# Graph attention softmax: the carry into a row's first and last run by two operations with tables of 16-bit penalties instead of a second pair of scans

## The reference

```python
q = (x @ Wq + bq).reshape(n, H, C)          # n = 6250, H = 4, C = 64
kj = (x @ Wk + bk).reshape(n, H, C)[src] + (edge_attr @ We).reshape(-1, H, C)
vj = (x @ Wv + bv).reshape(n, H, C)[src] + (edge_attr @ We).reshape(-1, H, C)
logits = einsum('ehc,ehc->eh', q[dst], kj) / sqrt(C)
m = segment_max(logits, dst)
ex = exp(logits - m[dst])
a = ex / (segment_sum(ex, dst)[dst] + 1e-16)
agg = segment_sum(vj * a, dst).reshape(n, H * C)
h = relu(agg + x @ Ws + bs)                  # and the same once more on h, without relu
```

## Time and profile before

| what | value |
|---|---|
| time, median of 3 runs | 4497.03 us (4490.62 to 4498.63) |
| the profiled execution's own time | 4498.7 us |
| its span, from first to last instruction | 4496.9 us |
| busy share of the span | PE 91%, DVE 84%, ACT 68%, POOL 71% |
| DMA | 237 GB/s mean, about 250 GB/s in the attention passes |

### The profile page before, as it was taken

How to read it: one execution, slowest core, us unless ns; L and a number is a source line. 1 busy time by engine, 2 the same in 40 slices (tenths; PEclk the granted TensorE clock), 3 DMA queues, 4 the chain that set the end, 5 groups by cost and what they waited for, 6 DMA issues and landing times. The chain is left out here.

```text
span 4496.9 us, 108726 instructions
## 1 busy us (share of the span) xinstructions
PE 4109.7 (91%) x17720; PEld 3175.0 (71%) x17720; DVE 3759.8 (84%) x20610; ACT 3036.2 (68%) x10782; POOL 3210.1 (71%) x3078
## 2 busy tenths in 40 slices
PE   5999999998979999999999998979999999999996
PEld 4887877775657777777777775557777777777764
DVE  5655555556979999999999998889999999999996
ACT  2333333333518988889898895139999999999983
POOL 6777777773067888778787782188888888888842
PEclk9999999999999999999999999999999999999999
DMA  5887887774678888888888884588888888888855
GB/s 171 255 250 236 247 242 241 237 234 134 204 235 257 260 257 256 255 253 258 259 261 250 253 265 122 181 253 259 259 255 255 257 258 255 256 259 256 260 156 160
DMA packets 770941, 1064.81 MB, mean 237 GB/s; under 512 B 111323, under 2 KB 588728, under 8 KB 770277
## 3 DMA queue, kind: packets, MB, share of 16 engines
q0 software_dynamic: 171184, 540.40, 40.1%
q1 hardware_dynamic: 599094, 517.47, 38.1%
HBM read 906.27 MB, written 151.16 MB: 235 GB/s over the span
## 5 line engine op out<-in xcount | busy, mean ns | idle before, releaser
L1476 POOL DMA_INDIRECT e_kv<-kv,src x1664 | 1662.6, 999 | 536.7 <-issue 301.1
L1709 ACT ACTIVATE e_vals<-e_kvj,e_ex 128x65 f32<-128x65 f32 x6572 | 1686.7, 334 | 0.1
L1497 PE MATMUL e_q<-q,e_pick 128*128 x3328 | 1056.2, 399 | 144.7 <-DVE e_logit L1604 113.7
L1604 DVE CUSTOM_DVE_ANT_0 e_kvj<-e_kvj,e_q 128x64 f32<-128x64 f32 x6656 | 1062.7, 215 | 4.3 <-PE e_q L1497 0.4
L153 POOL DMA_INDIRECT rows_x<-x_rows,rows_src x783 | 745.2, 952 | 243.5 <-issue 174.3
L1497 PEld LDWEIGHTS e_q<-q,e_pick 128*128 128x128 f32 x3328 | 576.6, 190 | 434.7 <-issue 369.4
L1539 PE MATMUL e_sum<-e_vals,e_mask 128*128 128x260 f32 x2536 | 784.8, 391 | 20.4 <-ACT e_vals L1709 9.4
L1592 DVE TENSOR_TENSOR e_kvj<-e_kv,e_e 128x512 f32<-128x512 f32 x1110 | 752.8, 678 | 54.9 <-DMA e_kv<-kv,src 28.6
L1487 PE MATMUL e_e<-e_we,e_ea 112*128 112x256 f32 x2220 | 670.6, 383 | 39.4 <-DMA e_ea<-attr_tiles 39.3
L1468 POOL TENSOR_SCALAR e_pick<-e_spots,own 128x512 f32<-128x512 bf16 x416 | 688.5, 1655 | 17.8 <-DMA e_spots<-locals 4.3
L1665 DVE TENSOR_TENSOR acc<-acc,e_sum 128x260 f32 x1602 | 668.5, 417 | 33.9 <-PE e_sum L1539 22.8
(11 more groups left out here) (226 smaller groups left out, 4904.3 us busy)
## 6 DMA issues: line engine op xcount, KB each, us to landing
e_ea<-attr_tiles SPq DMA_DIRECT2D x1110, 112.0 KB
edges<-q SPq DMA_DIRECT2D x277, 256.0 KB
e_made<-edges SPq DMA_DIRECT2D x554, 128.0 KB
e_spots<-locals SPq DMA_DIRECT2D x416, 128.0 KB
q<-attr_tiles SPq DMA_DIRECT2D x277, 112.0 KB
e_kv<-kv,src POOLq DMA_INDIRECT x1664
e_plain<-masks SPq DMA_DIRECT2D x396, 64.0 KB
masks<-q SPq DMA_DIRECT2D x208, 64.0 KB
```

Source lines behind the costliest of these rows:

```text
L1476: e.indirect_dma_start(out=kv[:, u, :], out_offset=None, **rows_of(kv_rows, k["src"][:, i:i + 1])).then_inc(kv_got[u], 16)
L1497: e.matmul(pe_q[i % 2][:, 0:D], pick[:, c, at:at + P], rows, start=True, stop=True).then_inc(q_done, 1)
L1604: dot = e.tensor_tensor_reduce(kvj[:, i % 2, h, 0:C], kvj[:, i % 2, h, 0:C], pe_q[i % 2][:, hs], 1.0, 0.0, ALU.mult, ALU.add, logit[:, j % ...
L1709: by_weight = e.activation(vals[:, n % R, h * HV:(h + 1) * HV], kvj[:, 2 + n % NV, h, :], ACT.Copy, scale=ex[:, b % 2, h, r:r + 1])
```

## The change

In step 5 the two scans are replaced by two elementwise operations. What comes into a row from the left can only reach the row's first run of equal destinations, and it can be added there without a scan if a table says for each edge whether it still belongs to the first run: `reach[..., 0, :]` is the running minimum of the penalties from the left (0 in the first run, -2^100 behind it), `reach[..., 1, :]` the same from the right. Both are 16-bit (bf16). The setup makes them by 14 scans and stores them to a new table `reaches` with 7 DMAs; each batch loads them by four more DMAs of SP (160 instead of 96 counts on the semaphore); and ACT now makes `ends` in two operations instead of one, since it adds the link penalty of each side.

```diff
@@ make_tables, SP
                 e.dma_start(quads[:].rearrange("p a s -> p (a s)"),
                             quad_table.rearrange("a s -> (a s)").unsqueeze(0)).then_inc(quads_got, 16)
+                for g in range(G):
+                    e.wait_ge(reached, 2 * g + 2)
+                    e.dma_start(reaches[g * P:(g + 1) * P, :], reach[:, g % 4, :, :].rearrange("p a c -> p (a c)")).then_inc(reach_stored[g % 4], 16)
                 e.wait_ge(linked, 6)
@@ make_tables, DVE
                 take_sources(G - 1)
+                e.memset(reach[:, :, 0, 0:1], 0.0).then_inc(ends_clear, 1)
+                e.memset(reach[:, :, 1, P - 1:P], 0.0).then_inc(ends_clear, 1)
+                e.wait_ge(ends_clear, 2)
+                for g in range(G):
+                    if g >= 4:
+                        e.wait_ge(reach_stored[g % 4], 16 * (g // 4))
+                    e.tensor_tensor_scan(reach[:, g % 4, 0, 1:P], pen[:, g, :], pen[:, g, :], 0.0, ALU.min, ALU.bypass).then_inc(reached, 1)
+                    e.tensor_tensor_scan(reach[:, g % 4, 1, 0:P - 1][:, ::-1], pen[:, g, ::-1], pen[:, g, ::-1], 0.0,
+                                         ALU.min, ALU.bypass).then_inc(reached, 1)
                 e.wait_ge(quads_got, 16)
@@ edge_pass_attention, SP, load_runs
                     for h in range(H):
                         e.dma_start(pen[ROWS * h + 1:ROWS * h + 1 + BATCH, j % 2, :],
                                     pens[j * BATCH:(j + 1) * BATCH, 0:P + 1]).then_inc(runs_got[j % 2], 16)
+                        e.dma_start(reach[ROWS * h + 1:ROWS * h + 1 + BATCH, j % 2, :, :].rearrange("p a c -> p (a c)"),
+                                    reaches[j * BATCH:(j + 1) * BATCH, :]).then_inc(runs_got[j % 2], 16)
@@ edge_pass_attention, DVE
+                e.memset(reach[:], 0.0).then_inc(cleared, 1)
...
                     elif step == 5:
                         e.wait_ge(ends_down, j + 1)
                         e.wait_ge(mx_inner, j + 1)
-                        forward(j, ends[:, 0:1]).then_inc(fw_done, 1)
+                        e.scalar_tensor_tensor(fw[:], reach[:, j % 2, 0, :], ends[:, 0:1], mx[:], ALU.add, ALU.max).then_inc(fw_done, 1)
                         e.wait_ge(fw_done, 2 * j + 2)
                         e.wait_ge(ends_up, j + 1)
-                        backward(j, ends[:, 1:2]).then_inc(mx_done, 1)
+                        e.scalar_tensor_tensor(mx[:], reach[:, j % 2, 1, :], ends[:, 1:2], fw[:], ALU.add, ALU.max).then_inc(mx_done, 1)
@@ edge_pass_attention, ACT, step 4
-                        e.activation(ends[:], back[:, P:P + 2], ACT.Copy).then_inc(ends_down, 1)
+                        e.wait_ge(runs_got[j % 2], 160 * (j // 2 + 1))
+                        e.activation(ends[:, 0:1], back[:, P:P + 1], ACT.Identity, bias=pen[:, j % 2, 0:1], scale=1.0)
+                        e.activation(ends[:, 1:2], back[:, P + 1:P + 2], ACT.Identity, bias=pen[:, j % 2, P:P + 1],
+                                     scale=1.0).then_inc(ends_down, 1)
```

More of the change, by code:

```diff
@@ L160, in gathered, with make_tables @@
         e.wait_ge(self.got[i // self.GANG % self.gangs], 16 * many)
-def make_tables(nc, k, t, s, pens, locals16, singles, ring):
+def make_tables(nc, k, t, s, pens, reaches, locals16, singles, ring):
     G, B, S = s.groups, s.blocks, s.table
@@ L212, in make_tables @@
         pen = ph.sb("pen", [P, G, P - 1])
+        reach = ph.sb("reach", [P, 4, 2, P], BF16)
         quad_rows = ph.sb("quad_rows", [5 * G, P])
@@ L257, in _ @@
                 e.wait_ge(stored, 16 * (2 * G + 3))
+                for u in range(4):
+                    e.wait_ge(reach_stored[u], 16 * len(range(u, G, 4)))
             @block.gpsimd
@@ L1270, in _, with edge_pass_attention @@
                         tools.root(e, b)
-def edge_pass_attention(nc, name, k, t, s, w_edge, edge_rows_made, masks_made, kv_rows, pens, locals16, singles, skip_of, last):
+def edge_pass_attention(nc, name, k, t, s, w_edge, edge_rows_made, masks_made, kv_rows, pens, reaches, locals16, singles, skip_of, last):
     PACE = 2
@@ L1313, in edge_pass_attention @@
         pen = ph.sb("pen", [P, 2, P + 1])
+        reach = ph.sb("reach", [P, 2, 2, P], BF16)
         lr = ph.sb("lr", [P, 2, P])
@@ L1417, in load_runs @@
                     if j == 0:
-                        e.wait_ge(cleared, 7)
+                        e.wait_ge(cleared, 8)
                     if j >= 2:
@@ L1606, in dots @@
                     dot.then_inc(dots_done, 1)
[L1608 to L1613, removed]
                 def softmax(j, step):
@@ L1625, in softmax @@
                             e.wait_ge(edge_rows, j)
-                        backward(j, -BIG).then_inc(mx_inner, 1)
+                        e.tensor_tensor_scan(mx[:, ::-1], pen[:, j % 2, 1:P + 1][:, ::-1], fw[:, ::-1], -BIG,
+                                             ALU.add, ALU.max).then_inc(mx_inner, 1)
                     elif step == 3:
@@ L1763, in build @@
     pens, locals16 = scratch("pens", [s.table, P + 2]), scratch("locals16", [s.table, P], BF16)
-    singles = scratch("singles", [2, s.table])
+    reaches, singles = scratch("reaches", [s.table, 2 * P], BF16), scratch("singles", [2, s.table])
     (w_skip1, b_skip1), (w_skip2, b_skip2) = ((t[f"w_proj{c}"][:, :, 3 * D:], t[f"b_proj{c}"][:, 3 * D:]) for c in (1, 2))
@@ L1771, in build @@
             with Phase(nc, "e0") as ph:
-                begun = make_tables(nc, k, t, s, pens, locals16, singles, ring)
+                begun = make_tables(nc, k, t, s, pens, reaches, locals16, singles, ring)
                 edge_pass_weighted(nc, ph, k, t, s, ring, begun, own, edges, masks, first)
             node_pass_resnorm(nc, k, s, first, x1, kv[0], cols[0])
-        edge_pass_attention(nc, "e1", k, t, s, t["w_edge1"], edges[:, 0:D], masks, kv[0], pens, locals16, singles,
+        edge_pass_attention(nc, "e1", k, t, s, t["w_edge1"], edges[:, 0:D], masks, kv[0], pens, reaches, locals16, singles,
                             (cols[0], w_skip1, b_skip1, skip), None)
@@ L1779, in build @@
             last = LastRows(outer, k, cols[1], x1, w_skip2, b_skip2)
-            edge_pass_attention(nc, "e2", k, t, s, t["w_edge2"], edges[:, D:2 * D], masks, kv[1], pens, locals16, singles,
+            edge_pass_attention(nc, "e2", k, t, s, t["w_edge2"], edges[:, D:2 * D], masks, kv[1], pens, reaches, locals16, singles,
                                 None, last)
```

5 lines of the change are left out of this document (3 added, 2 removed).

## The result

The changed kernel takes 4515.67 us (median of 7 runs, 4507.46 to 4526.7), the kernel before 4495.9 us on the same chip: ratio 1.0047, 95% interval 1.0034 to 1.006. It is **20 us slower**, where I had forecast no difference.

The account below looks back on a forecast made before the run. DVE was taken to pace the first pass, POOL the second. First pass -8.8 + 6.6 = -2.2 us, second 0, setup 0, from 4498.7 to 4496.5, less 1.7 for the median: 4495 us, range 4480 to 4508.

Parts of the forecast that it names:

- SP's burst comes too late in both passes: Rival: loads behind line 1446's burst come late, 13 us a pass minus first pass's 8.8; 4514 us, chance 0.10.
- Step 5's price: DVE, step 5: new operations take 344 ns against scans of 480 and 484, gaining 8.8 us a pass.
- the rival built on that rule: Rival: step 5's new operation costs what a scan does, 477 ns; 4502 us, chance 0.05.
- Who paces: DVE paces the first attention pass, POOL the second at 1.697 us a tile, with some 3 us to give.
- sum of fixed steps: POOL, second pass: 0.305 us ahead of gathers, 0.17 behind masks, 222 of 225.1 us idle.
- I count 0 of 8.8 us: Second pass: DVE's step 5 gain only lengthens its wait for gathered rows, so none of it arrives.
- SP's queue: Four more issues a batch on SP, 52 us a pass, mostly hidden: 6.6 us in the first pass, 0 in the second.
- 52 x 0.13 = 6.6 us in the first pass: SP's 52 us of added issues, at 0.13 us of DVE for each us of SP, cost 6.6 us.
- my upper bound (26 us): Bound on SP's queue cost: twice the rate of 0.13, in both passes, 26 us.
- the sign that I had named: Sign of a wrong forecast: an `e_ea` wait of tens of us in the second pass, from SP's burst.
- In the second pass SP is ahead: Second pass: DVE stalls from SP's issues stay below what POOL holds it anyway, so they cost 0.
- ACT, setup, the rest: ACT's second operation, a setup 2.4 us late, one memset and 3.4 MB more to load: all hidden, 0.

Follow-up runs that it names:

- e15: Kernel before with step 5's two new operations on one column, one ACT copy, reach loaded for two batches a pass only: 0.9964 on the first chip.
- e6: Changed kernel with reach stored behind the penalties in the same row, so six issues a batch instead of ten: 0.9982 of the kernel before.
- e18: Repeat of e6, reach in the penalties' table with six issues a batch: 0.9975 of the kernel before.
- e13: Kernel before plus the loads of reach, unused, with the old scans and single ACT operation: 1.0057 on the first chip.
- e17: Changed kernel with five attribute buffers instead of four in the second pass: 4510.97 us, 1.0033 of the kernel before.
- e8: Changed kernel with reach loaded for the first two batches of a pass only and one ACT copy, without link penalties: 0.9988 on the first chip.
- e5: The changed kernel itself, measured again on a chip like the first: 1.0036 of the kernel before.
- e16: Changed kernel with its ten loads a batch spread over ten tiles instead of in a row: 0.9968 on the first chip.
- e7: As e6, reach in the penalties' table, with the six issues spread over six tiles: 0.9981 of the kernel before.
- e1: Kernel before plus the loads of reach, unused, with the old scans and single ACT operation: 1.0033 on the slow chip.
- e9: Repeat of e1, the unused loads of reach added to the kernel before: 1.0031 on the slow chip.
- e11: The kernel before, unchanged, run again for a second profile: 0.9994.

## Why the prediction was wrong

**Which outcome.** It was the rival "SP's burst comes too late in both passes", which I had put at 4514 us with a chance of 0.10; 4515.67 was measured. That the rival's price agrees so well is in part luck: it has nothing for step 5 in the second pass and 13 us of stalls in each, where the first pass got 18 us of stalls and the second 7.

**Step 5's price: right.** I took 344 ns, measured 348 and 352. The price of a column is now measured too: the same operations on one column take (e15)

```profile
L1652 DVE SCALAR_TENSOR_TENSOR e_fw<-e_reach,e_ends,e_mx x64: 205/216/768, 1329.9 to 4322.5; 128x1 f32<-128x1 bf16 x64
```

and 219 ns, so 127 columns are (348 - 216) / 127 = 1.04 ns each. The Trainium skill, "Vector Engine (DVE) Microarchitecture Reference", section 7, gives half throughput to two non-bf16 sources; the mixed pair here takes 1.04 ns a column, as good as the 1.03 worked out for two fp32 sources, so the trace shows none of it, and the rival built on that rule is out.

**Who paces: right; what follows from it: half right.** POOL paces the second pass of the kernel before, as I had it, and its sum of fixed steps holds to 3 us in every version without the burst. Two things do not follow from it. With the burst in place DVE holds the second pass too (POOL waits 5 to 8 us), and there step 5's gain counts: "In the second pass ... I count 0 of 8.8 us" is wrong for the kernel that I was asked about. And the floor is not a constant: with one table the second pass is 3 to 9 us shorter than before, since POOL's masks take 8 to 20 ns less and its gathers 999 and 1005 ns (e6, e18). The whole kernel gains 8 and 11 us there by the ratios, near my 8.8, but not as I had counted it: the first pass is 13 to 19 us shorter by the profiles, of which step 5 explains 8.4, and the rest of the kernel is longer. One reading was incomplete: DVE's larger waits in the first pass sum to 63 us and not 48, for line 1665 waits 14.4 us for PE's sums beside the 14.4 of line 1661. Nothing else hangs on it.

**SP's queue: the step that failed.** The term that failed is "52 x 0.13 = 6.6 us in the first pass", and 0 in the second. The issue time in it was right: I had 1.62 us a batch, the bursts grew from 2.96 to 4.62 us. Three things behind it were wrong. First, the rate, "0.13 us of DVE for each us of SP", came from dividing a pass's waits by SP's hold; measured are 25.7 us (e13) for 64 x 1.66 = 106 us of issues, 0.24, which is my upper bound (26 us) and not the value that I took (6.6). That the store of line 496 makes made rows late was right, and these waits are still there, unchanged.

An average can't give the price of a burst: a load is late or not by whether the row of issues ahead of it eats up its lead. That lead was 6.3 us in the median of the first pass, against 4.8 us that a made row takes to come; the change moved it to 4.7. Second, I looked at the wrong load: the next attribute load, 5.15 us behind the burst with three others in front of it, did not set the end (e17), though it did become late: PE waits 20.5 us for it in the second pass, the sign that I had named, and loses nothing by it. What cost time was the made row, with a ring of two, directly behind the burst or up to four loads further on. Third, "In the second pass SP is ahead", and so 0: being ahead on average did not help a load whose buffer comes free only three tiles before its use.

In the numbers: first pass, gain 8.4 us, DVE's wait for late rows +18.3 us (+15.1 in the second pair of profiles), together +7 to +10 us; the passes of the two pairs are 9.7 and 6.0 us longer.

**ACT, setup, the rest: right.** ACT's two operations (241 and 244 ns) are hidden (e8 against e6 and e18); the setup ends at 59.1 us as against 59.8; the bytes cost nothing that shows (e6).

Together: 25.7 us for the issues, less 8 to 11 us for step 5, is 15 to 18 us; the changed kernel was measured at +16 (e5) and +20 us.

**Open.** That the made rows are the late load is read from the traces; what a third buffer for them would give back was not run. Why POOL's gathers and masks take longer in one version than in another, and with it why the floor of the second pass moved, isn't known; e16's second pass shows no gain because its gathers took 1010 ns. Why the first pass became 5 to 10 us shorter than step 5 explains, in e6, e7, e16 and e18 alike, isn't known either. On the slow chip the made rows behind the bursts are late as well, but less often (4 and 7 batches of the first pass in e1 and e9, 11 us; none in e11), and the loads cost about half. There DVE waits more for PE's sums, so something else already holds it; that this is the reason was not tested.

## What to carry to other kernels

Price additional issues on a DMA queue by the longest run of issues in a row against the shortest lead of what stands directly behind it (issue to use, less the time that the transfer needs), and look first at the ring with the fewest buffers. Look at the next few loads as well and not at the first alone: 8 of the 13 late rows had others between them and the burst. A rate of waits over a whole pass says little about it. Four issues that cost 26 us in a row cost nothing that shows when spread over tiles, or when their bytes ride on transfers that are there anyway: here new columns belonged into an existing table. And where one engine paces a stage by its own instructions, the length of the stage follows their mean duration, which is to be read again after each change. The Trainium skill, "Perfetto Trace Analysis", section "What 'DMA-bound' means", names an issuing sequencer that is solid with DMA slices as a bound; here it was solid for 4.6 us in every 45, and that was enough.

## What the runs showed of the hardware

The kernel before, unchanged, takes 4494 to 4502 us in some groups of runs and 4975 to 4977 us in others, 10.6% more, at granted clocks of about 0.986 and 0.973. What differs with it is what the DMAs move: 189 GB/s against 237 in the weighted sum, 240 and 236 against 257 in the two passes (e11), while DVE is as busy as before (3774 and 3760 us). The effects kept their signs on both, but not their sizes (the loads: +0.57% and +0.32%).

Four issues take 1.65 us of SP with 26 rows of 516 bytes and also with 26 rows of 1028: doubling the bytes of a row left the burst at 2.95 us (e18, median). A load of 128 rows by SP had its last semaphore count 4.4 to 4.8 us behind the start of its issue in the median of a pass, of which the issue itself was 0.42 us. POOL's step ahead of a gather was 0.305 us behind another gather and 0.17 behind a mask in the profiles of both kinds, while the gathers themselves took 999 to 1010 ns (second passes of the first kind).
